# Max pass of the attention: the causal mask of query tiles 2 and 3 added by VectorE instead of a matmul

## What is computed

```python
scores = einsum('bhid,bhjd->bhij', q, k) / 4          # 16 heads of 16 dimensions
scores = scores - slope[h] * (i - j) where j <= i, -inf where j > i
attn = softmax(scores); x1 = layernorm(x + (attn @ v) @ Wo + bo)
hidden = silu(x1 @ ternary(W_up).T) * (x1 @ ternary(W_gate).T)
out = layernorm(x1 + hidden @ ternary(W_down).T)
```

## Time and profile before

| | us |
|---|---|
| median of 3 runs | 677.17 |
| lowest, highest | 676.7, 678.27 |
| the profiled execution, device time | 679.84 |
| its span, first to last instruction | 678.0 |
| TensorE busy in it | 601.9 |
| VectorE busy in it | 510.7 |
| ScalarE, GpSimd busy in it | 306.7, 303.8 |

### The profile page before, as it was taken

The page is one execution under the profiler, slowest core; times in us unless marked ns, Lnnn a source line. Parts: engine busy times, 40 slices in busy tenths (PEclk is TensorE's granted clock), DMA queues, the critical chain, the costliest instruction groups (busy, mean ns, idle before and its releaser), DMA issues.

```text
span 678.0 us, 13169 instructions
## 1 busy us (share of the span) xinstructions
PE 601.9 (89%) x4322; PEld 353.6 (52%) x4322; DVE 510.7 (75%) x1015; ACT 306.7 (45%) x543; POOL 303.8 (45%) x492
## 2 busy tenths in 40 slices
PE   4186798999989998999989998999989998999694
PEld 2043345565556645565546655565556645565443
DVE  3264875998689876988689876988689876987454
ACT  1024452358424662358324662358324762358141
POOL 0113973355443563445443563455443563345323
PEclk9677999999999999999999999999999999999988
DMA  6765117601553027601563027601563027601000
GB/s 170 153 219 94 33 57 147 141 2 35 140 132 68 1 86 147 139 1 38 139 135 60 1 86 147 139 1 38 137 136 62 1 86 147 139 1 54 11 0 32
DMA packets 35808, 56.85 MB, mean 84 GB/s; under 512 B 4784, under 2 KB 31920, under 8 KB 32688
## 3 DMA queue, kind: packets, MB, share of 16 engines
q1 hardware_dynamic: 35792, 56.64, 36.0%
HBM read 39.59 MB, written 16.78 MB: 83 GB/s over the span
## 4 chain that ended last, share of the span: by engine, by line
PE 57%; DVE 18%; DMA 16%; issue 4%; SPq 2%; POOL 2%; ACT 1%; POOLq 0%; DVEq 0%; ACTq 0%
PE ring L529 16%; DMA k_stack<-qk_scratch 11%; PE max_bank L452 10%; PE acc L542 7%; PE ring L469 7%; PE acc L482 5%; PE max_bank L454 4%; DMA qk_scratch<-qk_parts 3%; DVE neg_max L695 3%; PE ring L432 3%; DVE x L634 3%; DVE qk_rest L673 2%; DVE qk_rest L664 2%; DVE qk_parts L671 1%; DVE qk_parts L675 1%
## 5 line engine op out<-in xcount | busy, mean ns | idle before, releaser
L695 DVE TENSOR_REDUCE neg_max<-max_bank 128x1 f32<-128x384 f32 (+3 forms) x352 | 213.5, 633 | 43.6 <-PE max_bank L454 40.7
L584 ACT ACTIVATE probs<-ring 128x512 f32<-128x512 f32 x320 | 170.5, 604 | 100.6 <-PE ring L469 98.0
L816 POOL TENSOR_SCALAR_AFFINE_SELECT probs<-probs 128x256 f32<-128x256 f32 (+1 forms) x320 | 121.7, 409 | 103.1 <-ACT probs L584 102.2
L452 PE MATMUL max_bank<-k_stack,q_stack 112*128 112x384 bf16 (+3 forms) x512 | 134.7, 307 | 31.0 <-DMA k_stack<-qk_scratch 26.2
L846 POOL TENSOR_TENSOR hidden_lo<-hidden,hidden_hi 128x512 f16<-128x512 f32 x64 | 73.7, 1158 | 129.5 <-ACT hidden_hi L614 129.5
L469 PE MATMUL ring<-q_stack,k_stack 128*128 128x512 bf16 (+3 forms) x512 | 102.5, 303 | 2.0 <-DMA q_stack<-max_parts 1.3
L454 PE MATMUL max_bank<-causal,ident_bf 128*128 128x128 bf16 x512 | 101.4, 224 | 0.0
L452 PEld LDWEIGHTS max_bank<-k_stack,q_stack 112*128 112x128 bf16 x512 | 50.4, 99 | 72.4 <-DVE neg_max L695 20.0
L603 ACT ACTIVATE gating<-ring,tanh_scale 128x512 f32<-128x512 f32 x64 | 44.0, 687 | 89.5 <-PE ring L529 89.5
L482 PE MATMUL acc<-probs,v_ones 128*32 128x512 f32 (+3 forms) x1024 | 79.4, 440 | 3.0 <-POOL probs L816 2.9
L432 PE MATMUL ring<-x_t,wqkv 128*128 128x512 f32 x128 | 64.4, 630 | 5.6 <-DVE x_t L658 5.6
(11 more groups left out here) (89 smaller groups left out, 836.5 us busy)
## 6 DMA issues: line engine op xcount, KB each, us to landing
qk_scratch<-qk_parts SPq DMA_DIRECT2D x32, 384.0 KB, 2.6
q_stack<-qk_scratch SPq DMA_DIRECT2D x16, 384.0 KB, 4.9
k_stack<-qk_scratch SPq DMA_DIRECT2D x16, 384.0 KB, 7.1
xin<-x_dram SPq DMA_DIRECT2D x9, 512.0 KB, 8.9
q_stack<-qk_scratch SPq DMA_DIRECT2D x16, 256.0 KB, 5.8
k_stack<-qk_scratch SPq DMA_DIRECT2D x16, 256.0 KB, 8.0
res<-x_dram SPq DMA_DIRECT2D x8, 512.0 KB, 3.9
out_dram<-y SPq DMA_DIRECT2D x8, 512.0 KB, 3.2
```

Source lines behind the costliest of these rows:

```text
L452: pe.matmul(o, q_stack[0:MAX_ROW, 4 * g + h, P * tile:P * (tile + 1)], k_stack[0:MAX_ROW, 4 * g + h, 0:width], start=True, stop=False)
L584: rg.drained(act.activation(probs[:, g % 2, n, :], rg.bank(step)[:, :], ACT.Exp), step)
L695: dve.tensor_reduce(neg_max[:, g, first_col:first_col + 4 * (len(heads) - 1) + 1:4], max_bank[k][:, 0:width * len(heads)].rearrange("p (h ...
L816: return pool.affine_select(out=v, in_=v, compare_op=ALU.is_ge, fill=0.0, base=0, pattern=([[0, blocks]] if blocks > 1 else []) + [[1, P]] ...
```

## The change

For query tiles 2 and 3, the wide units, the mask matmul goes: the score matmul alone fills the bank and signals `max_filled`. VectorE's `take` of such a unit becomes a `tensor_tensor_reduce`: it reads the scores from PSUM and a new bf16 tile `causal_wide` (zero but for the mask in its last 128 columns) from SBUF, adds them, multiplies by -1, writes the result back over the scores, and takes the minimum into `neg_max`, starting from 3e38. Ahead of it stands an increment of a semaphore that nobody waits for, which carries the wait on `max_filled`. GpSimd fills `causal_wide` at the start. The narrow units 0 to 2 stay as they were, and so does the order of steps.

```diff
@@ TensorE, step max
-                            pe.matmul(o, q_stack[0:MAX_ROW, 4 * g + h, P * tile:P * (tile + 1)],
-                                      k_stack[0:MAX_ROW, 4 * g + h, 0:width], start=True, stop=False)
-                            mm = pe.matmul(o[:, width - P:width], ident_bf[:, :], causal[:, :], start=False, stop=True)
+                            mm = pe.matmul(o, q_stack[0:MAX_ROW, 4 * g + h, P * tile:P * (tile + 1)],
+                                           k_stack[0:MAX_ROW, 4 * g + h, 0:width], start=True, stop=tile >= MASK_BY_DVE)
+                            if tile < MASK_BY_DVE:
+                                mm = pe.matmul(o[:, width - P:width], ident_bf[:, :], causal[:, :], start=False, stop=True)
                         mm.then_inc(max_filled[k], 1)
@@ VectorE, step take
                         at_least(dve, max_filled[k], MAX_PER_BANK, it, use + 1)
                         first_col = 4 * heads[0] + tile
+                        if tile >= MASK_BY_DVE:
+                            dve.sem_inc(dve_passed, 1)
+                            scores = max_bank[k][:, 0:width]
+                            dve.tensor_tensor_reduce(
+                                scores, scores, causal_wide[:, SEQ - width:SEQ], -1.0, LOWEST_START, ALU.add, ALU.min,
+                                neg_max[:, g, first_col:first_col + 1]).then_inc(max_drained[k], 1)
+                            continue
                         dve.tensor_reduce(
@@ GpSimd, at the start
+            pool.memset(causal_wide[:, :], 0.0).then_inc(pool_step, 1)
-            pool.wait_ge(pool_step, 2)
+            pool.wait_ge(pool_step, 3)
...
+            pool.affine_select(out=causal_wide[:, SEQ - P:SEQ], in_=causal_wide[:, SEQ - P:SEQ], compare_op=ALU.is_ge,
+                               fill=MASKED, base=0, pattern=[[-1, P]], channel_multiplier=1).then_inc(pool_step, 1)
-            pool.wait_ge(pool_step, 4)
+            pool.wait_ge(pool_step, 6)
             pool.tensor_copy(ident_bf[:, :], ident[:, :]).then_inc(consts_set, 1)
```

More of the change, by code:

```diff
@@ L28 @@
 MASKED = -1e30
+LOWEST_START = 3e38
 HIDDEN_SCALE = 0.25
@@ L38 @@
 RING = 4
+MASK_BY_DVE = 2
 EXP_UNITS = 10
@@ L163, in block_kernel @@
         causal = sb("causal", [P, P], BF16)
+        causal_wide = sb("causal_wide", [P, SEQ], BF16)
         ones = sb("ones", [P, P], F32)
```

## The result

The changed kernel took 683.97 us (median of 4 runs, 682.16 to 687.22) against 677.72 for the kernel before on the same occasion: a ratio of 1.0094, 95% interval 1.0049 to 1.0139. Run once more with more repetitions it took 683.29 against 679.68: 1.0063, interval 1.0044 to 1.0081, or +4.3 us (3.0 to 5.5; the medians lie 3.6 apart). Both say slower; the second is the sharper one, and the forecast's +6.7 lies inside the first interval and above the second. So the sign and the order of the change are as forecast, and its size was put too high; how much of the agreement is luck stands further down.

A forecast was written before the change was run, and what follows sets the result against it. TensorE was taken to carry the chain with VectorE nearly full beside it. +0.8 us a pass, +5.6 in seven passes and +1.1 in the first gave +6.7: 683.9 us on the median, range 670 to 708.

The forecast's parts named there:

- A: Loop pass, 277.3 to 290.6 us: VectorE has no room, nine takes at 0.07 plus later release, +0.7 us.
- C: Loop pass, 300.9 to 315.4 us: half of twelve takes' 0.84 us on VectorE counted, +0.4 us.
- TensorE's part: Mask matmul slots saved on TensorE: 32 of 0.057 us, 1.8 us a pass, at most 14.6 us over the run.
- The main instruction: VectorE's new wide take: no slot change, as in the swish row; upper end 0.22 us more.
- The read of the minimum: Separate accumulator read after each wide take on VectorE: slot 0.07 us, bank released 0.07 us later.
- The wait: Wait on a separate increment ahead of VectorE's take: 0.1 us for each of 7 waits a pass, mostly hidden.
- B: Loop pass, 290.6 to 300.9 us: VectorE has 1.5 us idle, TensorE gives back 0.5 less some 0.2; lag then +0.4 us.
- Lead-in: Loop pass, 267.2 to 277.3 us: VectorE gains 3 to 4 slots against 0.75 us idle, 0 to +0.1 us.
- the first batch: The first pass with its 32 wide takes: 0.07 us for half of the takes, +1.1 us.
- Faster: Rival: the minimum costs no slot of its own on VectorE, 670.5 us; chance 0.17.
- The held read: Rival: the accumulator read waits for the main instruction, +0.15 to +0.24 us a take, 704 to 727 us; chance 0.20.
- The slow write: Rival: writing into the bank being read slows VectorE's main instruction by 0.22 us, 729 us or above; chance 0.05.

The follow-up runs named there:

- the old takes: Mask matmuls of the wide units removed from the kernel before, VectorE's reductions kept: 673.17 us, ratio 0.9916.
- takes 0.13 us lighter: Kernel before with all matmuls, each wide take leaving out the first 128 columns: 675.82 us, ratio 0.9956.
- the first three kernels: Against the kernel before: the change again, 683.29 us; new takes with all mask matmuls kept, 688.02; wide units' mask matmuls removed with reductions kept, 673.17.
- the carrier: Kernel before with only the semaphore increment that carries the wait added ahead of each wide take: 681.43 us, ratio 1.0040.
- VectorE's half: Kernel before with the new instruction in the wide takes, all 512 mask matmuls kept: 688.02 us, ratio 1.0140.

## Why the prediction was right, and where it was off

**What bounds.** The reading that both engines are nearly full in A and C, and that the saved slots would turn into waits, holds: 1.1 to 5.5 us of waits in a pass, and half of TensorE's gain lost even with the old takes. The deeper reading, that VectorE has no room in A and its slots pass on there one to one, does not: with takes 0.13 us lighter A stayed at 13.04 us, with TensorE busy throughout. TensorE set the pace, and VectorE stood close behind. What fits all runs is a round trip over two banks: the take starts, the bank is released, TensorE fills. The theories of the first three kernels said that VectorE paces, and their ranges were met; that doesn't show it, since two engines that hold each other give the same. That a later start costs time with no more work on VectorE is shown by the carrier (0.28 in a pass). That the round trip and not VectorE's busy time is what limits the changed kernel is argued, not shown: lighter takes shorten both, and no run had a third bank.

**TensorE's part.** 32 x 0.057 = 1.8 us in a pass was right as the ceiling. It came back as 0.92 with the old takes, and as 77.01 - 76.28 = 0.73 with the new.

**The main instruction.** I took no change and kept 0.22 as the upper end. It is 0.023 longer, and its slot 0.04 more where it stands right behind another of its kind (0.65 against 0.61). The step that failed here is "I take nothing, since swish is the nearest row": swish writes to SBUF. With the write to SBUF the row is near the swish's (688 ns against 681 in the changed kernel's trace), and the cost of the write back is 0.44 us in a pass.

**The read of the minimum.** That there is one, as ScalarE's row suggested, was right. Its slot was put at 0.07 and is 0.01 ahead of other work; its duration, 0.15 to 0.16, measured 0.14, and the release, 0.07 later, was right. The term of the sum that was mis-sized is this one: 32 x 0.07 = 2.2 us of slots in a pass, where the rows give 32 x 0.01 = 0.3 for single takes and would give 32 x 0.05 = 1.6 if each stood behind another.

**The wait.** I put in 0.1 for each of 7 waits, mostly hidden in B. The price of one was right (0.11 later with the carrier alone, 0.16 in the changed kernel). That it hides was not: the carrier alone costs 0.28 in a pass. And "where a bank was filled in time this costs nothing" fails at the end of quad 3, where the take starts 0.12 later behind a short operation. So this term was undersized, as the read was oversized.

**The stretches.** A was to lose 0.7 and lost 13.39 - 13.30 = 0.09, or 0.15 from take to take: this is where the slot of 0.07 on an engine without room went wrong, nine times. B was to give back 0.3 and gave 0.2. C was to lose 0.4 and lost 0.43, but not by the twelve slots of 0.07 that stood in the sum: that it agrees is luck. Lead-in: 0 to 0.1, measured 0.15. In C the six takes at the end show both terms (timeline of VectorE):

```profile
313.06 0.17 DVE L652 TENSOR_SCALAR var_eps<-mean_var 128x4 f32<-128x4 f32 x1
313.31 0.57 DVE L702 CUSTOM_DVE_ANT_0 max_bank<-max_bank,causal_wide 128x384 f32<-128x384 f32 x1
...
317.23 0.14 DVE L702 DVE_READ_ACCUMULATOR2_ANT neg_max<- 128x1 f32 x1
```

The first starts 0.25 after the operation ahead of it (0.09 before), and the six last from 313.31 to 317.37, 4.06 against 3.81: 0.16 and 0.25, nearly all that C lost. The loss of a pass thus sits in the one place where six takes follow each other with no other work of VectorE between them. A pass lost 0.41 instead of 0.8, and six passes 2.5 instead of 4.8. For the first batch I put 1.1; what is left beside the six passes is 1.1 to 1.8, with a scatter of over 1 us. So the forecast of 6.7 came near 4.3 with an oversized read and an undersized wait and write back, which made up for each other in part: the coupling of the two engines was foreseen, the prices agree by luck. The constants that GpSimd makes cost nothing: TensorE's first transpose starts at 4.53 us, 4.54 before.

**The rivals.** Faster, because the minimum costs no slot: the slot is indeed nearly free (0.61 against 0.60), and the kernel is slower all the same, by start and write, and with them the later release. This rival's condition nearly held and its result did not, the plainest sign that the forecast's price stood in the wrong place. The held read is out: the next operation starts with the read. The rule of the Trainium skill that the next operation waits until the pipe has emptied (page "VectorE: DVE Perf Modes", section "The DRAIN you can't avoid"), which the same section limits to operations that are held, does not describe these rows: the next start lies before the main instruction's end each time (282.38 against 281.77 + 0.69 = 282.46). Its section "Two Vector instructions with no wait between them", by which the instruction counts as two and neither is held, agrees with them. The slow write had the right mechanism and a price of 0.22 where 0.02 (the row) to 0.04 (the slot behind another) was measured.

**What stays open.** The parts of VectorE's half, 1.14 us in a pass with the masks on and 1.33 with them off, are the carrier (0.28, masks on) and the write back (0.44, masks off); 0.4 to 0.6 is left for the read and its release, if the parts add, and no kernel measured these alone. Whether the round trip over two banks or VectorE's work limits the changed kernel is open too, and the time ahead of the loop's second pass is known only with its scatter.

## What to carry to other kernels

When one engine hands a buffer to another through two banks, price a changed instruction also by when it can start and when it releases, and not only by its slot: here the slot grew by 0.01 to 0.05 us, the release came 0.07 later and the start behind a fill 0.16 later, and together they cost 1.1 us in a pass of 32 takes. Being busy nearly all the time doesn't make an engine the bound: taking 4.2 us of work from VectorE gave 0.28. Here half of the matmul slots' time came back at best (0.92 of 1.8 us) while the takes stayed as they were. Better than moving work is to ask whether it is needed: a mask in a pass that only finds the shift of a softmax could go entirely on the inputs used here, for 1.5% of the kernel.

## What the runs showed of the hardware

- A `tensor_tensor_reduce` on VectorE shows as two instructions; the accumulator's read starts 0.61 us after the main one of 512 columns, where the old take's next operation started after 0.60, and the next operation starts together with the read. The read lasts 140 ns when the main instruction wrote to PSUM, 82 when it wrote to SBUF.
- With 512 float32 columns the main instruction lasts 706 ns when it writes back into the PSUM bank that it reads, 688 when it writes to SBUF.
- A one-column fill on VectorE behind a 512-column reduction shows at 0.02 us after the next operation's start and takes no slot, while two such tiny operations in a row stand 0.07 apart.
- Behind a wait that sits on a separate increment a take starts 0.15 us after the fill's end, behind one that sits on the instruction 0.04. With no wait to be served, it starts 0.21 against 0.09 after a short operation's start, and at the same time as before behind one with a slot of 0.60.
